# Turning the values on VectorE and through DRAM, beginning six output blocks ahead of the last item, and moving GpSimd's power behind three more weight splits

## The reference, cut to what matters

```python
x = x + _L0_conv_ref(_gn(x), ...)   # lambda layer: q, k, v by 1x1 products, softmax over k, relative positions
x = x + _L1_conv_ref(_gn(x), ...)   # 16 heads of 64, causal (8 heads) and anti-causal (8 heads) masks, per image pair
x = x + _L2_conv_ref(_gn(x), ...)   # 16 heads of 64, biases on q, k, v, relative-position terms added to the scores
x = x + _L3_conv_ref(_gn(x), ...)   # 3x3 depthwise filter, then a tensor-train product of 1024 x 1024, relu

# the attention that both middle layers compute, for each head:
p = softmax(q @ k.T * scale + terms)
o = p @ v
out = concat(o) @ Wo + b
```

## Time and profile before

| | us |
|---|---|
| median of 3 runs | 1272.16 (1270.01 to 1274.7) |
| the profiled execution, as timed | 1270.89 |
| its span, first to last instruction | 1269.1 |
| TensorE matmuls busy | 1223.5 (96%) |
| VectorE busy | 695.7 (55%) |
| GpSimd busy | 640.6 (50%) |
| ScalarE busy | 475.2 (37%) |
| mean granted TensorE clock | 0.991 of full speed |

### The profile page before, as it was taken

The page is one execution under the profiler, slowest core; times in us unless marked ns, Lnnn a source line. Parts: engine busy times, 40 slices in busy tenths (PEclk is TensorE's granted clock), DMA queues, the critical chain, the costliest instruction groups (busy, mean ns, idle before and its releaser), DMA issues.

```text
span 1269.1 us, 19561 instructions
## 1 busy us (share of the span) xinstructions
PE 1223.5 (96%) x6768; PEld 979.7 (77%) x6768; DVE 695.7 (55%) x1434; ACT 475.2 (37%) x1229; POOL 640.6 (50%) x726
## 2 busy tenths in 40 slices
PE   6999999999999998999999899999989999889998
PEld 4788895478888876888878678778768787668887
DVE  7633454865664523565552477756337777567312
ACT  3611241135553501555540065544204655343312
POOL 4623399165555565555556455555654555454000
PEclk9999999999999999999999899999999999999999
DMA  5211123025555442455545246656524566620011
GB/s 181 82 50 42 43 56 104 9 82 177 147 159 166 140 139 78 127 172 144 165 136 158 75 150 187 204 160 215 165 75 148 158 188 201 184 80 1 22 45 67
DMA packets 129377, 155.05 MB, mean 122 GB/s; under 512 B 30080, under 2 KB 84000, under 8 KB 129280
## 3 DMA queue, kind: packets, MB, share of 16 engines
q1 hardware_dynamic: 118976, 146.92, 38.7%
q10 hardware_dynamic: 10304, 6.88, 1.8%
HBM read 111.81 MB, written 37.75 MB: 118 GB/s over the span
## 4 chain that ended last, share of the span: by engine, by line
PE 83%; DVE 7%; issue 4%; ACT 3%; DMA 1%; POOL 1%; SPq 1%; ACTq 0%; POOLq 0%; DVEq 0%
PE PS L1137 49%; PE PS L682 7%; PE PS L1757 7%; PE PS L1183 3%; PE PS L960 3%; PE PS L969 2%; PE PS L975 2%; PE PS L1774 2%; PE PS L1227 2%; PE PS L1216 2%; PE PS L1247 1%; PE PS L665 1%; PE PS L1197 1%; DVE PS L1481 1%; DVE part L1538 1%
## 5 line engine op out<-in xcount | busy, mean ns | idle before, releaser
L1137 PE MATMUL PS<-XB,w_hi 128*128 128x512 f32 x1024 | 343.6, 400 | 10.0 <-POOL w_lo L228 10.0
L226 POOL CAST w_hi<-w_raw 128x512 fp32r<-128x512 f32 x195 | 123.9, 635 | 305.8 <-PE PS L1137 220.0
L228 POOL TENSOR_TENSOR w_lo<-w_raw,w_hi 128x512 fp32r<-128x512 f32 x195 | 255.5, 1310 | 15.6
L1137 PEld LDWEIGHTS PS<-XB,w_hi 128*128 128x128 f32 x1024 | 194.1, 190 | 57.2 <-POOL w_lo L228 9.6
L1137 PE MATMUL PS<-XB,w_lo 128*128 128x512 f32 x512 | 201.7, 394 | 0.0
L1137 PE MATMUL PS<-XB,part 128*128 128x512 f32 x768 | 192.9, 398 | 4.4 <-POOL part L228 4.4
L1137 PEld LDWEIGHTS PS<-XB,part 128*128 128x128 f32 x768 | 143.5, 190 | 37.5 <-POOL part L228 4.8
L1372 ACT ACTIVATE part<-PS,nmax 128x256 f32<-128x256 f32 (+1 forms) x256 | 112.2, 443 | 141.3 <-DVE nmax L1484 92.9
L1137 PE MATMUL PS<-part,w_hi 128*128 128x512 f32 x344 | 113.0, 395 | 3.8 <-DVE part L1543 1.5
L1382 ACT ACTIVATE part<-part,prec 128x256 f32<-128x256 f32 (+1 forms) x256 | 105.8, 475 | 27.5 <-DVE prec L1499 27.5
L228 POOL TENSOR_TENSOR part<-part,part 128x512 fp32r<-128x512 f32 x85 | 111.6, 1313 | 6.8
(11 more groups left out here) (136 smaller groups left out, 1889.8 us busy)
## 6 DMA issues: line engine op xcount, KB each, us to landing
w_raw<-in_w SPq DMA_DIRECT2D x187, 256.0 KB, 2.7
part<-in_w SPq DMA_DIRECT2D x85, 256.0 KB, 2.8
turned<-part SPq DMA_DIRECT2D x128, 128.0 KB, 2.9
part<-turned SPq DMA_DIRECT2D x32, 512.0 KB, 5.2
turned<-part SPq DMA_DIRECT2D x128, 96.0 KB, 2.4
part<-turned SPq DMA_DIRECT2D x32, 384.0 KB, 3.9
strips<-part ACTq DMA_DIRECT2D x16, 256.0 KB, 2.7
out_x<-xT SPq DMA_DIRECT2D x16, 256.0 KB, 2.1
```

The lines of the kernel that those rows point to most:

```text
L226: pool.tensor_copy(hi, raw).then_inc(w_hi_done, 1)
L228: pool.tensor_tensor(lo, raw, hi.bitcast(F32), ALU.subtract).then_inc(w_ready, 1)
L1137: m = nc.tensor.matmul(PS[:, bank, :], wt[:, (c % 4) * P:(c % 4) * P + P], rhs(hl, c), start=c == k == 0, stop=c == CK - 1 and k == 2)
```

## The change

The values no longer pass TensorE. VectorE transposes them in 32 x 32 blocks straight out of the PSUM bank of the product V into `vB` (`turn_values`), ScalarE's queue writes `vB` to DRAM with four DMAs (`values_to_dram`) at the place where `evac_v` stood, and reads it back in the next item behind `evac_q` with one DMA (`values_from_dram`); ScalarE then copies `vB` into `v` in another order of blocks (`take_v`), behind the exponentials of the first two score blocks and before their division. The bias of v is added to o instead. The output blocks of a stage no longer wait as a whole for the values to be taken: block 0 waits for o alone, block 1 for the bank of V. GpSimd's power of stages 1 to 3 stands behind three more splits. In the tail, blocks 1 to 4 run over chunks 0 to 3 before attend 31 and block 5 behind it, each of the six in a bank of its own, and the products `build_m` are dealt out anew.

```diff
-            for o in {ITEMS - 2: (0,), ITEMS - 1: (1, 2)}.get(i, ()):
+            for o in {ITEMS - 2: (0,), ITEMS - 1: (1, 2, 3, 4, 5)}.get(i, ()):
                 take((3, "O", o), 2, "O", o, (0,))
         for o in range(CK):
-            take((3, "O", o), 2, "O", o, (1,) if o < 3 else range(2))
+            take((3, "O", o), 2, "O", o, (1,) if o < 6 else range(2))
...
+    values = nc.dram_tensor("values", (2, P, 4 * P), F32).ap()
...
-    M_AFTER = {(0, 1): (), (1, 1): (0, 1), (2, 1): (2, 3), (3, 0): (4,), (3, 1): (5, 6),
-               (4, 0): (7,), (4, 1): (8, 9), (5, 0): (10, 11), (5, 1): (12,), (6, 0): (13,), (6, 1): (14,), (7, 0): (15,), (7, 1): ()}
+    M_AFTER = {(5, 0): (0, 1), (0, 1): (2,), (1, 1): (3, 4), (2, 1): (5,), (3, 1): (6, 7), (4, 1): (8,),
+               (5, 1): (9, 10), (6, 0): (11, 12), (6, 1): (13,), (7, 0): (14, 15), (7, 1): ()}
+    M_BANKS = (S + 3, O)
...
                 if c == 0 and kind == "V" and i:
-                    pe.wait_ge(v_evac, i)
+                    pe.wait_ge(v_turned, i)
...
-        def turn_values(i):
-            pe.wait_ge(v_evac, i + 1)
...
-            for tt in range(4):
-                m = nc.tensor.transpose(PS[:, turned_bank(i), tt * P:tt * P + P], vT[:, tt * P:tt * P + P], ident[:, :])
-            m.then_inc(v_tr, 1)
...
-                if c == 0 and s < 3 and o < 2:
-                    i = PAIRS * (s + 1)
-                    pe.wait_ge(o_hi, i)
-                    pe.wait_ge(o_lo, i)
-                    pe.wait_ge(v_evac, i + 1)
+                if c == 0 and s < 3 and o == 0:
+                    pe.wait_ge(o_hi, PAIRS * (s + 1))
+                    pe.wait_ge(o_lo, PAIRS * (s + 1))
+                if c == 0 and s < 3 and o == 1:
+                    pe.wait_ge(v_turned, PAIRS * (s + 1) + 1)
...
         scores(LAST, 1)
-        out_block(3, 0, range(0, 2))
-        turn_values(i)
-        out_block(3, 0, range(2, 4))
+        out_block(3, 0, range(0, 4))
         project(LAST, "V", range(CK))
         attend(i, 0)
         attend(i, 1)
-        out_block(3, 1, range(0, 4))
-        turn_values(LAST)
-        out_block(3, 2, range(0, 4))
-        for o in range(3):
-            out_block(3, o, range(4, 7))
+        for o in range(1, 5):
+            out_block(3, o, range(0, 4))
         attend(LAST, 0)
         attend(LAST, 1)
-        for o in range(3):
-            out_block(3, o, range(7, CK))
+        out_block(3, 5, range(0, 4))
+        for k in M_AFTER[5, 0]:
+            build_m(k)
+        for o in range(6):
+            out_block(3, o, range(4, CK))
...
     def attention_act(act):
-        def evac_v(i):
...
+        def take_v(i):
+
+            act.wait_ge(v_in, 16 * (i + 1))
             if i:
-                act.wait_ge(v_tr, i)
...
+                act.wait_ge(o_done, 2 * i)
+            dst = v.rearrange("p t (b c) -> p t b c", b=4)
+            nc.scalar.activation(dst, vB.rearrange("p (b t c) -> p t b c", b=4, t=4), ACT.Copy).then_inc(v_ready, 1)
...
             if i:
                 evac_q(i + 1)
+                if i < LAST:
+                    values_from_dram(act, i - 1)
             exps(i, 0)
             exps(i, 1)
+            if i == LAST:
+                values_from_dram(act, i - 1)
+            elif i:
+                take_v(i - 1)
             normalize(i, 0)
...
             evac_k(i + 1)
             if j:
                 evac_o(i - 1)
-            evac_v(i)
+            if i < LAST:
+                values_to_dram(act, i)
             if 1 <= j <= 4:
                 for c in (2 * j - 2, 2 * j - 1):
                     norm.y(nc.scalar, s + 1, c)
...
-        def take_v(i):
-            dve.wait_ge(v_tr, i + 1)
+        def turn_values(i):
+
+            product_done(dve, (i, "V"))
             if i:
-                dve.wait_ge(o_done, 2 * i)
-            nc.vector.tensor_copy(v.rearrange("p a n -> p (a n)"), PS[:, turned_bank(i), :]).then_inc(v_ready, 1)
+                dve.wait_ge(v_ready, i)
+            src = PS[:, bank_of(i, "V"), :].rearrange("p (t q c) -> p t q c", t=4, q=4)
+            dst = vB.rearrange("p (q t c) -> p t q c", q=4, t=4)
+            nc.vector.transpose(dst, src).then_inc(v_turned, 1)
...
             if j:
                 rest_of_o(i - 1)
-            if i and j == 0:
-                take_v(i)
+            if i < LAST:
+                turn_values(i)
...
+    def values_to_dram(act, i):
+
+        act.wait_ge(v_turned, i + 1)
+        if i >= 2:
+            act.wait_ge(v_in, 16 * (i - 1))
+        for b in range(4):
+            to = bass.AP(values.tensor, (i % 2) * P * 4 * P + P * b, [[4 * P, 32], [32 * 4 * P, 4], [1, P]])
+            act.dma_start(to, vB[32 * b:32 * b + 32, :].rearrange("p (q r) -> p q r", q=4)).then_inc(v_out, 16)
+
+    def values_from_dram(act, i):
+        act.wait_ge(v_out, 64 * (i + 1))
+        act.dma_start(vB, values[i % 2, :, :]).then_inc(v_in, 16)
...
+            if n == PROBS_AT[LAST]:
+                probs_to_dram(sp, LAST, 0)
+                probs_from_dram(sp, LAST, 0)
+                probs_to_dram(sp, LAST, 1)
+                probs_from_dram(sp, LAST, 1)
...
-                if n == slots[(PAIRS * s + 2, "Q"), 0]:
+                if n == (slots[(PAIRS * s + 2, "Q"), 0] + 3 if s else slots[(2, "Q"), 0]):
                     norm.power(s + 1)
```

More of the change, by code:

```diff
@@ L1268, in out_block @@
                 if s == 3 and c == 0 and o == 1:
[L1269 to L1271 removed]
+                    pe.wait_ge(rel_evac, 2 * (ITEMS - LO_KEYS))
+                if s == 3 and c == 0 and 2 <= o < 5:
+                    pe.wait_ge(p_exp, 4 * LAST + o - 1)
+                if s == 3 and c == 0 and o == 5:
+                    pe.wait_ge(v_turned, ITEMS)
                 chunk_of((s, "O", o), c, lambda hl, c: (oh, ol)[hl][:, c, :], out_bank(s, o))
@@ L1300, in attention_pe @@
         project(0, "V", range(4, CK))
-        project(2, "Q", range(0, 2))
-        turn_values(0)
-        project(2, "Q", range(2, CK))
+        project(2, "Q", range(CK))
         for i in range(1, LAST - 1):
@@ L1311, in attention_pe @@
                 s = i // PAIRS - 1
-                out_block(s, 0, range(0, 2))
-                turn_values(i)
-                out_block(s, 0, range(2, CK))
-                for o in range(1, CK):
+                for o in range(CK):
                     out_block(s, o, range(CK))
-                project(i + 2, "Q", range(CK))
-            else:
-                project(i + 2, "Q", range(0, 2))
-                turn_values(i)
-                project(i + 2, "Q", range(2, CK))
+            project(i + 2, "Q", range(CK))
         i = LAST - 1
@@ L1454, in attention_act @@
                     norm.head(s + 1, c)
+        values_from_dram(act, LAST)
+        take_v(LAST)
         evac_o(LAST)
@@ L1598, in attention_dve @@
                 norm.group_stats(s + 1)
-            if j or i == 0:
-                take_v(i)
             if j == 0:
@@ L1608, in attention_dve @@
         rest_of_o(LAST)
+        for k in M_AFTER[5, 0]:
+            rest_of_m(dve, k)
         for o in range(CK):
-            for k in M_AFTER.get((o, 0), ()):
-                rest_of_m(dve, k)
+            if o >= 6:
+                for k in M_AFTER[o, 0]:
+                    rest_of_m(dve, k)
+                for k in (2 * o - 12, 2 * o - 11):
+                    stats_of(3, k)
             add_out(3, o)
-            if o:
-                stats_of(3, o - 1)
             for k in M_AFTER[o, 1]:
                 rest_of_m(dve, k)
-        stats_of(3, CK - 1)
+        for o in range(4, CK):
+            stats_of(3, o)
         norm.aggregate(5, range(CK), 16)
@@ L1655, in probs_from_dram @@
         sp.dma_start(probT[:, a, 0:w], turned[i % 2, a, :, 0:w]).then_inc(p_in[a], 16)
-    PROBS_AT = [slots[(i + 1, "K"), 0] + 8 if i < LAST else slots[(i, "V"), 0] + 7 for i in range(ITEMS)]
+    def values_to_dram(act, i):
[8 more added lines that the diff above has]
+        act.dma_start(vB, values[i % 2, :, :]).then_inc(v_in, 16)
+    PROBS_AT = [slots[(i + 1, "K"), 0] + 8 if i < LAST else slots[(i, "V"), 1] + 6 for i in range(ITEMS)]
     def attention_sp(sp):
@@ L1697, in attention_pool @@
                 masked_factor(pool, 2)
-            if n == slots[(3, "O", 5), 0]:
+            if n == slots[(3, "O", 5), 1]:
                 masked_factor(pool, 3)
```

71 lines of the change are left out of this document (34 added, 37 removed).

## The result

The changed kernel takes 1262.11 us (median of 11 executions, 1253.32 to 1267.78), the kernel before 1272.01 (1270.01 to 1274.7, 11 executions). The ratio is 0.9919, 95% interval 0.9899 to 0.9938: faster by 0.8%, 9.9 us, where 30 were forecast; the range ended at 1252. New is the spread too: 14 us, where the kernel before has 5. The chip showed a mean granted clock of 0.993 in it, and 0.984 to 0.995 in the others; the one of 1265.75 had 0.984.

A forecast was written before the change was run, and what follows sets the result against it. TensorE's matmuls, filling 96% of the span, were taken as the bound, with its idle times and clock. Gains of 43.2 us less 14.5 lost took 1270.9 to 1242 us; range 1228 to 1252.

The forecast's parts named there:

- E: Layer 2, eight items making the next stage's input: turn, DMA issues and take_v lengthen the ScalarE-VectorE loop; 12 us lost.
- F: Layer 2's attend: probabilities through DRAM come one or two tenths later in each of 16 items; 2.5 us lost.
- A: Every item: no transposes on TensorE, 0.44 us less in each of 32; 14.1 us gained.
- B: Stage boundaries: power behind three more splits removes TensorE's waits and the slow matmuls behind them; 20.3 us gained.
- C: Output blocks ahead of the values: waits for the values' copy out of PSUM and slow matmuls go; 4.3 us gained.
- D: The tail: two waits and a stretch at lower clock go, less two new waits; 4.5 us gained.
- The wait that was to be 1.0: In the tail: attend of item 31 waits for values or probabilities through DRAM, taken as 1.0 us.
- g: ScalarE's time to issue each of the four DMAs ahead of norm.y, 0.37 to 0.61 us.
- R2: Layer 2: each new wait before the relative products lowers the clock, 1.5 us each, 12 more lost, 1254; chance 0.10.
- the 1.39: A wait of TensorE in the earlier profile, behind which the next matmuls went at full speed; cited against R2.
- R3: Values' read lands too late for take_v and attend; slower, 1290 us at a landing of 8.5; chance 0.04.

The follow-up runs named there:

- e3: The changed kernel without the five DMAs of the values per item; ScalarE copies the turned blocks, not exchanged between partitions: 1226.42 us, ratio 0.9647.
- e1: The changed kernel timed and profiled once more, without any edit: 1258.75 us, ratio 0.9906.
- e2: The kernel before with only GpSimd's power of stages 1 to 3 moved behind three more splits: 1251.49 us, ratio 0.9845.
- e11: The kernel before with the power moved, output block 0 waiting for o alone and the transposes in block 1, values still on TensorE: 1243.73 us, ratio 0.9779.
- e4: The changed kernel with the five DMAs issued at their places, the read going to a second place and nobody waiting for it: 1250.03 us.
- e9: The changed kernel with VectorE's turn ahead of the rest of o and the four writes between norm.y and norm.head: 1237.15 us, ratio 0.9723.
- e12: As e4, nobody waiting for the values' read, but each DMA piece 64 B instead of 512 B: 1245.27 us.
- e7: The changed kernel with values written in 128 B pieces so that the read lands in v itself, without the copy take_v: 1271.54 us.

## Why the prediction was wrong

The direction and most sizes held; the sum of what the trip costs did not. The step that failed is the price of the trip, parts E and F: 14.5 in the sum, 35.7 between e3 and the changed kernel. Two things stood in it at nothing. One is the clock behind E's waits, which cost 6.4 in the profiled execution and 9.6 in e1's. The other is that `attend` waits in layer 1 too, 7.4 and 5.3. Term by term:

- **A** (14.1): items of layer 1 free of new waits went from 20.44 to 19.95, 0.49 x 32 = 15.7. Right, a little small.
- **B** (20.3): 19.9 in e2. Right, the clock's share included. The power was issued 0.3 later than before, counted from the scores of item 8 (64.3 to 64.6), and not 0.1; no cost of it shows.
- **C** (4.3): 7.8 between e2 and e11, of which 5.1 lie at the place that the part speaks of. Right, a little small. In the changed kernel itself the three items with output blocks took 222.6 from scores to scores and now take 197.8: 24.7 less; with the 1.2 of a new wait on line 1214 and without 1.5 of part A, 24.4 for B and C together, where they had 24.6.
- **D** (4.5): from the scores of item 31 to the end, the profiled execution went from 185.9 to 180.8, 5.1 with 0.4 of part A. The wait that was to be 1.0 is 3.64 in the profile, so that more than 4.5 was won elsewhere in the tail. The sum looks right and its parts are not. It is not sharp either: the tail of the kernel before, unaltered, took 185.3 in e2 and 182.7 in e11.
- **E** (12 lost): the mechanism, the place and g were right (0.45 to 0.69 per issue; waits of 9.2 and 10.4 before the relative products, present in e4, gone in e9). What was not in the term is the clock, 6.4 in the profile. This is rival R2, which I gave 0.10 on the strength of one row, the 1.39 after which the clock held. One row could not carry that. Before line 1234 the clock fell behind 0.75 and one wait of 0.77 in e1 and held behind the other 0.77; in e4 it held behind 1.48, 1.84, 2.12 and 2.43. So the length of one wait does not decide it, and what does is open. Per wait the forecast of R2, 1.5, was near (1.6, sometimes 3.2).
- **F** (2.5 lost): in layer 2 outside the tail 2.9, right. In layer 1 nothing was priced, because of this sentence in part E: "layer 1 has no relative products, and the rest of q is wanted only by the scores". True, and it led me to look at layer 1 no further. R3's room was worked out for layer 2 alone (14.4 us from V's end to `attend`, 2.4 to spare). In layer 1 the item is 1.8 shorter, and the copy of o and its rest take 1.1 each instead of 0.7, all ahead of the turn and the writes. `attend` waited there 5.3 for the values (gone in e4, which does not wait for them) and 2.1 for the probabilities.

The account of the profiled execution: 28.7 forecast, + 1.6 (A), + 2.8 (E, 12 - 9.2), - 6.4 (clock), - 7.4 (layer 1), - 0.4 (F in layer 2) = 18.9, and 17.6 was measured. The 1.3 between them I leave open.

The other 8.8, between that execution and the median, stay open for the most part. They come with the five DMAs, as e3's spread of 1.6 over four executions shows; with the DMAs issued and nobody waiting for the values e4 already spreads by 6.1. The mean clock accounts for about half at best: it is 0.989 in the median execution and 0.993 in the profiled one, and 0.004 x 1260 is 5. In e1 it does not order the executions (0.993 at 1262.24, 0.990 at 1254.26). There is no trace of one of the longer executions.

On the two pages that the prediction names. The Trainium skill, page "DMA: Bandwidth & Descriptors", section "Issuing engines are not separate DMA queues", pointed the right way: with ScalarE's transfers beside SP's the read of the probabilities lands in a median of 4.9 to 5.3 (changed kernel, e1, e4) instead of 4.4, though 4.7 of it is there in e3 without them, and e4 against e12 shows 4.4 more of waiting for it. The Trainium skill, page "TensorE: Matmul & The Clock Gate", section "A second HAM failure mode: psum-queue depth-cycling", says that frequent small gaps make the clock swing. The traces agree that it can fall behind gaps as small as 0.75, and show that it often does not.

## What to carry to other kernels

Work that leaves the busiest engine for a round trip through DRAM is bought with a deadline: write down, for every kind of item and not only for the tightest loop, when the data is made, what stands ahead of the issue on both engines, and when it is wanted. The instruction to put first is the one that starts the longest chain: one swap on VectorE and one on ScalarE were worth 22 to 25 us here (e9 against e1 and against the first result), and DMA issues belong where their engine is idle anyway. And try the parts of a change by themselves: the power's one line alone was better than the whole.

## What the runs showed of the hardware

- A copy in 128 B pieces landed later: writes of 64 KB took a median of 3.8 us so (e7) and 3.2 in 512 B pieces; four reads of 64 KB took a median of 5.9 us each so, and one of 256 KB in rows of 2 KB 4.5 us.
- The DMA engines were nearly full in these stretches before the change too. The kernel before, nine microseconds behind the scores of item 20:

```profile
791.60:794.60 3.00, 3.00 (x37) 2.61 (x34) 2.96 (x5) 0.00 (x0) 1.15 (x1) 1.00 0.89 216
794.60:797.60 3.00, 3.00 (x15) 2.48 (x14) 2.59 (x5) 2.02 (x9) 0.99 (x1) 1.00 1.03 370
797.60:800.60 3.00, 3.00 (x22) 2.02 (x22) 2.28 (x5) 2.24 (x8) 2.59 (x4) 1.00 0.46 144
```

The share (the column before the last) is 0.89, 1.03 and 0.46. With the change, the windows of item 20 above show 0.98, 1.00 and 0.97: no gap is left in these nine microseconds, though TensorE's wait of 2.43 also shifts what falls into them. The mean over the span, 122 GB/s on the page, shows nothing of it.
- An issue of a DMA of 32 partitions in 128 pieces took ScalarE 0.46 to 0.47 us, whether the pieces had 512 B or 64 B (e12); in 512 pieces of 128 B it took 0.55 (e7; all medians).
